# Fused transformer block: ScalarE issues a step's probabilities before the two operations of its gate

## The reference

```python
x = x + attn_a(layernorm(x))   # 16 heads of 8, RoPE on q and k, softmax over 256 keys
x = x + ffn(layernorm(x))      # h = silu(x Wg) * (x Wu); h Wd; 128 -> 384 -> 128
x = x + attn_b(layernorm(x))   # 16 heads of 8, causal, sparsemax over the keys
x = x + ffn(layernorm(x))      # the same weights
```

## Time and profile before

| | |
|---|---|
| Median of 3 runs | 612.29 (609.83 to 613.63) |
| Profiled execution, its time | 609.64 |
| Profiled execution, its span | 607.8 |
| Mean granted clock of TensorE | 0.992 of full speed |
| Busy: TensorE matmul | 575.9 (95%) |
| Busy: VectorE | 487.0 (80%) |
| Busy: ScalarE | 422.7 (70%) |
| Busy: GpSimd | 387.7 (64%) |
| Chain that ended last | TensorE 69%, VectorE 15%, issue 5%, ScalarE 3% |

### The profile page before, as it was taken

One profiled execution on the slowest core, in us unless ns is written; L12 is line 12 of the kernel. 1 busy time (PEld: TensorE's weight loads), 2 busy tenths in 40 slices (PEclk: granted clock), 3 DMA queues, 4 the chain that ended last, 5 costly groups with the idle time before them and its releaser, 6 DMA issues.

```text
span 607.8 us, 19101 instructions
## 1 busy us (share of the span) xinstructions
PE 575.9 (95%) x6680; PEld 445.2 (73%) x6680; DVE 487.0 (80%) x1426; ACT 422.7 (70%) x1057; POOL 387.7 (64%) x819
## 2 busy tenths in 40 slices
PE   8788999999999999999999999999999999999984
PEld 6555667777776777776777888777888888888663
DVE  3598889888898888888788887887888888899332
ACT  1115678777778777788888777777777787777762
POOL 4755568666767766777776766577676666653342
PEclk9999999999999999999999999999999999999996
DMA  7656655666565656555454533533644444450000
GB/s 222 187 142 159 162 157 141 155 142 147 152 176 142 168 141 148 128 152 138 127 136 129 139 98 97 126 95 84 145 108 115 119 122 110 117 128 19 12 10 22
DMA packets 74656, 76.24 MB, mean 125 GB/s; under 512 B 10348, under 2 KB 68908, under 8 KB 70092
## 3 DMA queue, kind: packets, MB, share of 16 engines
q1 hardware_dynamic: 63636, 68.09, 43.3%
q10 hardware_dynamic: 10920, 6.88, 5.4%
HBM read 46.86 MB, written 23.33 MB: 115 GB/s over the span
## 4 chain that ended last, share of the span: by engine, by line
PE 69%; DVE 15%; issue 5%; ACT 3%; DMA 3%; POOL 2%; SPq 1%; POOLq 0%; ACTq 0%; DVEq 0%
PE banks L1542 15%; PE banks L1496 10%; PE banks L1520 9%; PE banks L1470 7%; PE banks L1409 7%; DVE top L1114 4%; PE banks L1461 3%; DVE neg_shift L1108 3%; DVE top L1113 2%; PE banks L1499 2%; PE banks L1441 2%; PE banks L1462 2%; DMA k_stack<-k_image 2%; ACT probs_t L1305 2%; PE banks L1419 2%
## 5 line engine op out<-in xcount | busy, mean ns | idle before, releaser
L1305 ACT ACTIVATE probs_t<-banks 128x512 f32<-128x512 f32 (+1 forms) x512 | 266.8, 551 | 75.8 <-PE banks L1520 50.1
L1108 DVE TENSOR_REDUCE neg_shift<-banks 128x2 f32<-128x512 f32 x256 | 165.6, 680 | 33.5 <-PE banks L1496 32.2
L1542 PE MATMUL banks<-probs_t,v_ext 128*32 128x256 f32 (+1 forms) x2048 | 116.8, 357 | 0.0
L1496 PE MATMUL banks<-k_stack,q_stack 72*128 72x256 bf16 x512 | 98.9, 274 | 7.5 <-DVE neg_shift L1108 3.1
L1114 DVE MAX8 top<-banks 128x8 f32<-128x256 f32 x256 | 105.7, 413 | 0.0
L1520 PE MATMUL banks<-q_stack,k_stack 75*128 75x256 bf16 x512 | 98.4, 273 | 0.3 <-ACT probs_t L1305 0.2
L985 POOL TENSOR_TENSOR hidden<-up_tanh,gate_half 128x256 f32<-128x256 f32 x96 | 70.1, 732 | 42.9 <-DVE up_tanh L1154 42.7
L1113 DVE MAX8 top<-banks 128x8 f32<-128x128 f32 x256 | 74.2, 290 | 25.0 <-PE banks L1505 23.9
L1542 PEld LDWEIGHTS banks<-probs_t,v_ext 128*32 128x32 f32 x2048 | 55.3, 109 | 37.7 <-issue 13.0
L1496 PEld LDWEIGHTS banks<-k_stack,q_stack 72*128 72x128 bf16 x512 | 40.2, 97 | 46.8 <-DVE neg_shift L1108 35.4
L1499 PE MATMUL banks<-k_stack,q_stack 128*128 128x128 bf16 x256 | 56.6, 221 | 6.5 <-DVE top L1114 5.0
(11 more groups left out here) (115 smaller groups left out, 1377.3 us busy)
## 6 DMA issues: line engine op xcount, KB each, us to landing
q_stack<-q_image SPq DMA_DIRECT2D x93, 192.0 KB
k_stack<-k_image SPq DMA_DIRECT2D x93, 192.0 KB
q_image<-qk_parts SPq DMA_DIRECT2D x32, 192.0 KB, 2.3
k_image<-qk_parts SPq DMA_DIRECT2D x32, 192.0 KB, 2.1
q_image<-qk_parts SPq DMA_DIRECT2D x32, 128.0 KB, 2.2
o_image<-out_t SPq DMA_DIRECT2D x32, 128.0 KB, 1.8
out_compact<-o_image SPq DMA_DIRECT2D x32, 64.0 KB
rdenominators<-r_image SPq DMA_DIRECT2D x16, 128.0 KB, 3.5
```

What stands on the lines that cost most here:

```text
L1108: dve.tensor_reduce(m.nm[:, n % STACKS, h, :], scores.rearrange("p (q k) -> p q k", q=TT), AX.X, ALU.max, negate=True).then_inc(reduced, 1)
L1305: act.activation(m.pt[:, (n * Q + g) % GROUPS, i, 0:size], shifted_banks[:, j % 2, 0:size], ACT.Exp if is_soft(n) else ACT.Relu, scale=SCA ...
L1496: ins = pe.matmul(scores[:, qt * T:(qt + 1) * T], qs[0:STACK, h, qt * P:(qt + 1) * P], ks[0:STACK, h, :], start=True, stop=True)
L1542: ins = pe.matmul(out_bank[32 * i:32 * i + 32, at + skip:at + T], v_windows(v, kt)[:, Q * g + i, :], m.pt[:, (n * Q + g) % GROUPS, i, kt * ...
```

## The change

On ScalarE, within a step, the gate of the feed-forward is issued behind the layer norms and the probabilities, and no longer ahead of them. The instructions are the same, with the same operands and waits, and the order on every other engine stays.

```diff
                 if (n := due(step, "xT")) is not None:
                     take_xT(n)
-                for c in range(NC_H):
-                    if (n := due(step, f"gu{c}")) is not None:
-                        gate(n, c)
                 if (n := due(step, "a_norm")) is not None:
                     norm_a(n)
                 if (n := due(step, "f_norm")) is not None:
                     norm_f(n)
                 n, j = divmod(step - AT["pass2"], H)
                 if 0 <= n < ITEMS:
                     probs(n, j)
+                for c in range(NC_H):
+                    if (n := due(step, f"gu{c}")) is not None:
+                        gate(n, c)
```

## The result

The changed kernel takes 621.41 us (median of 4, 619.75 to 623.65) against 611.06 (median of 4, 608.44 to 613.63); the ratio is 1.0172, with a 95% interval of 1.0132 to 1.0213. The forecast was 621. It added 9.0 to the 612.29 of three runs; with the fourth the kernel before stands at 611.06, so the runs are 10.35 apart.

What follows compares the result with a forecast made beforehand. TensorE is busy nearly throughout and waits most often for VectorE's reductions, so VectorE's order sets its pace. The terms 3.9 + 4.5 + 0.9 - 0.3 = 9.0 us on the median 612.29 gave 621, range 614 to 626.

Steps and rivals of the forecast that it cites:

- Softmax items: Items 0 to 9: second gate ends 0.72 later, up_tanh and TensorE's first-pass product 0.39 later; 3.9 us in all.
- 0.23 at the front: ScalarE, start of a gate step's work: idles 0.23 longer, as probabilities must wait for their second-pass products.
- 0.39 of slack: Softmax item, VectorE: the second up_tanh starts 0.39 after its gate's end, so it has 0.39 to spare.
- hand-over: From the gate's end on ScalarE to up_tanh's start on VectorE: taken as 0.06, from TensorE's delay after the probabilities.
- Sparsemax items: Items 19 to 27: late up_tanh delays VectorE's reductions, and TensorE loses about 0.5 an item; 4.5 us in all.
- the third gate's part: Sparsemax item: the third gate's up_tanh at 508.61 instead of 508.04 delays the reductions that release TensorE; 0.37 forecast.
- the 0.52: Sparsemax item: delay of the reduction behind the third gate's up_tanh, 508.94 instead of 508.42, carried through to TensorE's release.
- Between: Items 10 to 18: up_tanh has more room; bounded by nothing and 0.39, taken as 0.1 an item, 0.9 us.
- End: Last items without first-pass products: earlier probabilities help TensorE; two items at -0.15, -0.3 us.
- Rival 1: TensorE's waits for probabilities: the wait removed is worth more than the wait added; full price 5.4 us, time 607; chance 0.04.
- Rival 2: Behind up_tanh: the gate's delay is taken up, no change; 3 us at most, 612 to 615; chance 0.14.
- Rival 3: Transition items cost the whole 0.39 and sparsemax items 0.65, more than forecast: 13 us, 625; chance 0.10.

Runs made afterwards that it cites:

- gu0 and gu1: The first and second gate of each item go behind the probabilities, the third stays ahead, against the kernel before: ratio 1.0121.
- gu1 alone: Only the second gate of each item goes behind its probabilities, against the kernel before: ratio 1.0054.
- gu0 alone: Only the first gate of each item goes behind its probabilities, against the kernel before: ratio 1.0081.
- gu2: Only the third gate of each item goes behind its probabilities, against the kernel before: ratio 1.0025.
- the old order with the later up1: Kernel before, with VectorE's second up_tanh of items 0 to 15 one step later, behind the next reduction: ratio 0.9989.
- the changed order with it: Changed kernel, with VectorE's second up_tanh of items 0 to 15 one step later: ratio 1.0112 to the kernel before.

## Why the prediction was right

**What bounds.** TensorE is held by VectorE's order in the stretch of the gates: shown, by the changed kernel's waits, and by taking up_tanh out of the way.

**Softmax items, 10 x 0.39 = 3.9.** Measured 0.38 or 0.39 in nine of them and 0.53 in the first; over steps 80 to 240 it is 4.0 (first-pass products at 97.14 and 276.21 before, 100.47 and 283.55 after). The chain on ScalarE was right to 0.01. Its parts are shown too: 0.23 at the front (gu0 and gu1 against gu1 alone), 0.49 for the added probabilities call (gu1 alone), 0.39 of slack. The hand-over from ScalarE to VectorE is 0.04, not 0.06. That 0.39 came out all the same has a little luck in it, since 0.37 follows with the shorter hand-over.

The estimate by the Trainium skill (ScalarE: Activation LUTs, What ACT_TABLE_LOAD costs) would have the second tanh 0.04 later than it came; the trace has 0.48 to 0.50 between starts around a softmax probabilities call, so the rows were the better price here.

**Sparsemax items, 9 x 0.5 = 4.5.** Measured 0.44 to 0.49 in the five steady ones, 0.22 and 0.64 in the first two and 0.72 and 0.65 in the last two (15.10 to 15.82 in the chain for the first of these); over steps 368 to 512 it is 4.5. The forecast of a steady item was 0.07 too high, in the third gate's part: from the end of that step's second-pass products to the release of TensorE it is 3.81 before (507.26 to 511.07) and 4.12 after (519.29 to 523.41), 0.31 more where 0.37 was forecast. The hand-over takes 0.03 of the difference, at 0.03 for 0.06, and VectorE's row of work from the reduction on most of the rest, at 2.61 for 2.65. That the 0.52 has the first gate's 0.15 in it was right: 0.15 and 0.29 alone, 0.45 together.

**Between, 9 x 0.1 = 0.9.** Over steps 240 to 368 the shift grows by 2.3, of which 1.4 is the clock's: 0.9. The 0.1 was a choice between two bounds, and that it gives the sum is luck as much as insight: the shifts go from 0.4 more to 0.15 less from item to item, and gu0 alone costs 0.44 in one of these items.

**End, -0.3.** From step 512 to 540 the shift falls from 14.16 to 13.85, 0.31 less. The weight loads' waits for the probabilities fall there from 3.7 to 3.0, which fits the reason given, but the gates alone don't behave alike: gu0 costs 0.4 in this stretch, gu1 0.5, and gu2 gives 0.65. The size was right, and the reason is not shown.

**The total.** The four parts add up to 9.1 measured, for 9.0. That the median then came within 0.4 of 621 is luck: the base of the forecast was 1.2 too high, and the runs differ by 1.3 more than the sum, of which the clock can be a part (0.985 to 0.992 in the four runs).

**Rivals.** Rival 1 had the right mechanism at 0.1 a softmax item, and the change as made hides it. Its full price was never to be had in the steady items: the 5.4 us are waits of the sparsemax heads' weight loads, and none of them lay in steps 368 to 511; the softmax heads' own (L1520) come to 0.3 us in steps 80 to 240, in a list that leaves out pauses as short as 0.1. The advice in the Trainium skill (Perfetto Trace Analysis, Optimization Strategy) holds here only once the second dependency is loosened: the old order with the later up1 and the changed order with it are 0.10 apart. Rival 2 is out, since nothing took the delay up. Rival 3's 0.65 a sparsemax item was reached in the last two and nearly in the second, but not in the steady ones, and the items between lost 0.1 each in the mean, not 0.39.

**Open.** What starts the stretches of half clock near 40 and near 55 us, which six of the twelve profiled executions have; the slow issue of the q_stack loads at step 304; and what the sparsemax items at the two ends of their stretch lose or gain beyond the steady ones.

## What to carry to other kernels

Before two calls of an in-order engine are swapped, find for each result the instruction that waits for it, how long it could still wait (from the producer's end to the consumer's start), and what is queued behind that consumer. Delays on the producer add up before they meet that slack, so halves of a change that cost nothing or little alone can cost the whole together. If the consumer can be put behind the work that matters, do that first; then look again whether the swap pays, and what the consumer's output was holding, a bank above all.

## What the runs showed that I had not expected

The granted clock fell to 1.2 GHz for 3 to 10 us early in several executions, in the changed kernel's behind 2 us in which TensorE did nothing (0.00 busy from 50 to 52). A pause there does not always bring it: the kernel before paused 1.16 us at the same product and kept full speed, and gu1 alone paused 0.82 and was at half speed 2 us later. Runs of the kernel before at a mean clock of 0.997 took 608 to 610 us, and those at 0.979 to 0.983 took 615 to 616. One execution can therefore be 4 us off the median, while the length of a steady item repeats to 0.02 between kernels and chips.
